# An early run of GpSimd's check, and four low halves of weights moved, in a fused attention and expert layer

## The reference, cut to what matters

```python
sim = jnp.einsum('bhnd,bhmd->bnm', Q, K) / (jnp.sqrt(jnp.float32(d)) * H)
k = max(1, int(n * TOP_K_RATIO))                      # 512 * 0.3
threshold = jax.lax.top_k(sim, k)[0][:, :, -1:]
A = jax.nn.sigmoid(sim) * (sim >= threshold)
A = (A + jnp.swapaxes(A, -1, -2)) * 0.5
x = x + (1 - gamma) * layernorm(x) + gamma * A
...
x = x + moe(layernorm(x)) + shared(layernorm(x))      # 8 experts, 2 per row; shared: silu(x sg + b) * (x su + b) @ sd
```

## Time and profile before

| | |
|---|---|
| runs | 503.43 us median of 3 (503.19 to 504.45) |
| span of the profiled execution | 502.5 us |
| busy: TensorE | 458.7 us (91%) |
| busy: VectorE | 330.9 us (66%) |
| busy: ScalarE | 259.6 us (52%) |
| busy: GpSimd | 148.8 us (30%) |
| mean granted TensorE clock | 0.972 of full |

### The profile page before, as it was taken

How to read it: one execution, slowest core, us unless ns; L and a number is a source line. 1 busy time by engine, 2 the same in 40 slices (tenths; PEclk the granted TensorE clock), 3 DMA queues, 4 the chain that set the end, 5 groups by cost and what they waited for, 6 DMA issues and landing times.

```text
span 502.5 us, 9186 instructions
## 1 busy us (share of the span) xinstructions
PE 458.7 (91%) x2649; PEld 257.1 (51%) x2650; DVE 330.9 (66%) x947; ACT 259.6 (52%) x490; POOL 148.8 (30%) x201
## 2 busy tenths in 40 slices
PE   7529899899999999999989999999999999999960
PEld 2215443455455445554445666666666666666630
DVE  3899989999999999659845555555555433333320
ACT  5899588288627852335445555554545333333320
POOL 3010100031002200410153554555455444444431
PEclk9778999999999999999999999999999999999995
DMA  7931420256023501355397798777777545445441
GB/s 264 277 78 54 136 85 1 83 113 162 0 85 87 83 0 66 109 83 146 107 188 234 187 226 197 181 178 198 176 176 180 87 67 100 83 76 93 82 68 23
DMA packets 39007, 60.55 MB, mean 121 GB/s; under 512 B 8234, under 2 KB 18730, under 8 KB 38963
## 3 DMA queue, kind: packets, MB, share of 16 engines
q0 software_dynamic: 10384, 23.38, 27.3%
q1 hardware_dynamic: 26514, 36.61, 23.1%
q10 hardware_dynamic: 2064, 0.02, 0.2%
HBM read 37.68 MB, written 22.30 MB: 119 GB/s over the span
## 4 chain that ended last, share of the span: by engine, by line
PE 76%; DVE 10%; DMA 4%; ACT 4%; issue 3%; POOL 1%; SPq 0%; DVEq 0%; POOLq 0%; ACTq 0%
PE bank L1055 6%; PE bank L1056 6%; PE bank L1057 6%; PE bank L1234 4%; PE bank L1238 4%; PE bank L1235 4%; PE bank L1210 4%; PE bank L1212 4%; PE bank L1214 4%; PE bank L1213 4%; PE bank L1215 4%; PE bank L1211 4%; PE bank L1067 3%; PE bank L1194 3%; PE bank L1070 3%
## 5 line engine op out<-in xcount | busy, mean ns | idle before, releaser
L567 POOL DMA_INDIRECT out_dram<-xb,sidx x35 | 55.9, 1597 | 83.8 <-ACT xb L905 65.0
L1055 PE MATMUL bank<-xT,W 128*128 128x512 f16 x176 | 66.8, 380 | 0.5 <-DVE sgt L1593 0.5
L1056 PE MATMUL bank<-xT,W 128*128 128x512 f16 x176 | 66.8, 379 | 0.0
L1057 PE MATMUL bank<-xT,W 128*128 128x512 f16 x176 | 66.8, 379 | 0.0
L1726 DVE TENSOR_TENSOR hS<-bank,hS 128x384 f16<-128x384 f32 x35 | 19.4, 556 | 67.9 <-ACT hS L897 67.9
L891 ACT ACTIVATE sgt<-bank 128x352 f32<-128x352 f32 x35 | 16.2, 462 | 72.9 <-PE bank L1215 72.9
L905 ACT ACTIVATE xb<-bank,wcol 128x512 f32<-128x512 f32 x35 | 24.0, 687 | 52.5 <-PE bank L1238 52.5
L1210 PE MATMUL bank<-W,xT 128*128 x140 | 43.8, 313 | 1.5 <-DVE W L1298 1.2
L1214 PE MATMUL bank<-W,xT 128*128 x140 | 43.8, 313 | 0.0
L1211 PE MATMUL bank<-W,xT 128*128 x140 | 43.8, 313 | 0.0
L1212 PE MATMUL bank<-W,xT 128*128 x140 | 43.8, 313 | 0.0
(11 more groups left out here) (263 smaller groups left out, 1022.4 us busy)
## 6 DMA issues: line engine op xcount, KB each, us to landing
out_dram<-W POOLq DMA_DIRECT2D x12, 256.0 KB, 5.1
stage<-L_ffn_down_w_in SPq DMA_DIRECT2D x12, 256.0 KB, 3.6
sim<-L_ffn_down_w_in SPq DMA_DIRECT2D x12, 256.0 KB
stage<-L_ffn_gate_w_in SPq DMA_DIRECT2D x16, 176.0 KB, 3.6
stage<-L_ffn_up_w_in SPq DMA_DIRECT2D x16, 176.0 KB, 4.5
sim<-L_ffn_gate_w_in SPq DMA_DIRECT2D x16, 176.0 KB
sim<-L_ffn_up_w_in SPq DMA_DIRECT2D x16, 176.0 KB
W<-x_in SPq DMA_DIRECT2D x2, 1024.0 KB, 6.8
```

What stands on the lines that cost most here:

```text
L567: pool.indirect_dma_start(out=out, out_offset=bass.IndirectOffsetOnAxis(ap=sidx[:, p:p + 1], axis=0), in_=y2[:, p, :], in_offset=None, com ...
L1055: pe.matmul(o, wh, xT[:, 0, c, :], start=(c == 0), stop=False)
L1056: pe.matmul(o, wh, xT[:, 1, c, :], start=False, stop=False)
L1057: last = pe.matmul(o, wl, xT[:, 0, c, :], start=False, stop=(c == KD - 1))
```

## The change

GpSimd, once its constants are set, runs the check instruction once on two columns of zeros (`bad[:, 2:4]`, used for nothing else). The low halves of units 8 and 9 are formed on TensorE (`form_down_low`, in place of four fillers behind the transposes of batch 0's normalised rows) and rounded by ScalarE (`round_down_low`). Those of units 10 to 13 stand in batch 1, one in each probe. The four squares of batch 1 move on ScalarE from ahead of the last four `round_low` to behind the two new roundings, ahead of the first count of batch 1, and `x_variance(1)` moves behind the low half in probe 0. The counts in the waits (`lows_done`, `s_wloA`) follow.

```diff
+PE_DOWN_LOWS = range(EARLY, EARLY + 2)
...
 def lows_done(n):
 
-    return n - len(PE_LOWS)
+    return n - len(PE_LOWS) - len(PE_DOWN_LOWS)
...
         pool.memset(hS[0:1, 1, SC - 1, :], 1.0).then_inc(s_const, 1)
+        link(pool.memset(bad[:, 2:4], 0.0))
+        pool.partition_all_reduce(bad[:, 3:4], bad[:, 2:3], P, bass.bass_isa.ReduceOp.max)
...
+        def round_down_low(i):
+
+            act.wait_ge(s_lowps, LOW_PARTS + i + 1)
+            lo = UNITS[PE_DOWN_LOWS[i]][2]
+            act.activation(W[:, lo:lo + D], bank[4 + i][:, :], ACT.Copy, scale=WS).then_inc(s_wloA, 1)
...
             x_mean(1)
-            for t in range(TB):
-                x_square(1, t)
             for f in range(4, LOW_PARTS):
                 round_low(f)
...
             x_hi(b, 2)
             x_hi(b, 3)
             if b == 0:
+                for i in range(len(PE_DOWN_LOWS)):
+                    round_down_low(i)
+                for t in range(TB):
+                    x_square(1, t)
                 count(1, 0)
...
+        def form_down_low(i):
+
+            n = PE_DOWN_LOWS[i]
+            pe.wait_ge(s_whi, n - EARLY + 1)
+            hi = UNITS[n][1]
+            pe.matmul(bank[4 + i][:, :], ident[:, :], staged(n)[0], start=True, stop=False)
+            pe.matmul(bank[4 + i][:, :], minus16[:, :], W[:, hi:hi + D], start=False, stop=True).then_inc(s_lowps, 1)
...
             if n == 0:
                 pe.wait_ge(s_wloD, KD)
-                pe.wait_ge(s_wloA, LOW_PARTS)
+                pe.wait_ge(s_wloA, LOW_PARTS + len(PE_DOWN_LOWS))
...
                 pe.wait_ge(s_wloA, LOW_PARTS)
-                keep_on(4)
+                for i in range(len(PE_DOWN_LOWS)):
+                    form_down_low(i)
             logits(b)
...
             if b == 1 and it == 0:
+                copy_logits(0)
+                weight_lo(10)
                 x_variance(1)
-                copy_logits(0)
-                weight_lo(12)
             if b == 1 and it == 1:
                 shared_hidden(0, 0)
                 layer_norm_x(1)
+                weight_lo(11)
             if b == 1 and it == 2:
                 shared_lo(0, 0)
-                weight_lo(13)
+                weight_lo(12)
             if b == 1 and it == 3:
                 shared_hidden(0, 1, lo_first=False)
+                weight_lo(13)
...
             link(dve.tensor_reduce(thr[:, :], pick[:, :, :], AX.X, ALU.add))
-            if b == 0:
-                weight_lo(8)
-                weight_lo(9)
...
-            if b == 0:
-                weight_lo(10)
-                weight_lo(11)
             dve.wait_ge(s_badr, b + 1)
```

## The result

| | before | after |
|---|---|---|
| median of 14 runs each, us | 503.81 (502.82 to 504.48) | 504.76 (503.77 to 505.38) |
| ratio, 95 % interval | | 1.0023 (1.0016 to 1.0030) |
| span of the profiled execution, us | 502.5 | 503.3 |

The changed kernel is slower by 0.23 % in the ratio of the runs, some 1.15 us; the two medians lie 0.95 us apart. I had forecast no visible change, 0.1 us the other way. The time lies in the range, but the direction was wrong. The loss is about the 0.7 to 1.05 us of rival B; B's time of 504.3 counted from the 503.43 of three runs, where the kernel before has 503.81 in fourteen.

A forecast was written before the change was run, and what follows sets the result against it. Bound: engines in turn until 89.66 us, with GpSimd's late check covered by VectorE's low halves, then TensorE. Span 502.5 - 1.17 (batch 0) + 1.05 (batch 1) = 502.38, plus 0.93 around it, 503.3 us; range 501.7 to 505.0.

The forecast's parts named there:

- rival B: GpSimd: each config change reloads the check; batch 0 gains 0 to 0.36, batch 1 loses 1.05; about 504.3 us; chance 0.18.
- Part 1: GpSimd's early run of the check: costs nothing, and batch 0's real check starts at 36.9 us in place of 39.58.
- the later price: GpSimd, batch 0: the check behaves as in later batches, starting right behind its flags at 36.9 us and taking 0.38.
- the other bound: GpSimd, batch 0: latest forecast start of the real check, 39.58 us, as in the kernel before; the early bound was 36.8.
- price of nothing: GpSimd's queue at the start: the early run is covered, free by 12 us, before the first wait ends at 32.36.
- Part 2: Batch 0's threshold without four low halves: VectorE gains 2.77 us, TensorE's fillers hold it to 41.91, batch 0 gains 1.17.
- Part 3: ScalarE, where batch 1's four squares (2.83 us) leave: nothing won, as the rounded parts behind them wait for TensorE.
- Part 4: Two low halves on TensorE and ScalarE: with the squares, batch 1's first count comes 0.9 us late; bounds 0 and 1.2.
- Part 5: VectorE's low halves between batch 1's probes: the one in probe 1 costs 0.15 us; batch 1 loses 1.05 in all.

The follow-up runs named there:

- experiment 1: The changed kernel without GpSimd's early run of the check; ratio to the kernel before 1.0021 (1.0009 to 1.0033).
- Experiment 7: The kernel before with one small GpSimd instruction between flags and check, a product in batch 1 and a memset in batch 2; single run 518.46 us.
- experiment 3: The changed kernel with batch 0's first-norm power left out of GpSimd's queue, VectorE using a straight line instead; ratio to the kernel before 0.9961.
- experiment 5: The changed kernel with VectorE's variance step of batch 0 one tile sooner; ratio to the kernel before 0.9988 (0.9972 to 1.0004).
- experiment 8: The changed kernel with batch 0's variance step one tile sooner and two of batch 1's four squares back in place; ratio to the kernel before 0.9972, median 502.53.
- experiment 4: The changed kernel with batch 1's four squares back ahead of ScalarE's last four rounded low parts; ratio to the kernel before 1.0006 (0.9991 to 1.0022).
- experiment 6: The kernel before with two of the four low halves put ahead of batch 0's flags; ratio to the kernel before 0.9989 (0.9972 to 1.0006).
- experiment 2: The kernel before with GpSimd's early run of the check alone added; ratio to the kernel before 0.9997 (0.9988 to 1.0005).

## Why the prediction was wrong

**Part 1 failed, at one price:** "I take the later price: start right behind the flags, at 36.9". It was 39.91, 0.33 past the other bound, 39.58, and rival B was the right case. (B's gain of 0 to 0.36 us for batch 0 did not come either: it was a loss of 0.14, less than the check's start scatters between traces.) Two readings led me wrong. I took the shorter checks of batches 1 to 3 (0.38 against 0.74 us) as a sign that the code stays loaded; experiment 1 shows a first check of 0.38. And I took prompt checks in batches 1 to 3 as the later price, though I had written that a wait of 19 us and more (18.6 in batch 3) would hide a load. Experiment 7 took that cover away and the load was there. The Trainium skill, GPSIMD Engine Reference, section Instruction dispatch, gives about 6 us for the first call of a freshly loaded kernel. These traces agree, with 5.59 to 6.13 us from the end of the power, and add that the check was fresh again after every config change that no long wait covered. The early run itself ended at 14.66 and not by 12, with a load of 8.94 us; it was covered all the same, so its price of nothing held.

**Part 2** was right as a mechanism and came to nothing with part 1. TensorE's hold by the fillers was seen in experiment 3, and with the check 1.31 us behind its flags (experiment 5) batch 0 gained 1.25 us on before at the transposes; I had 1.23. That the two agree so well is partly luck. I had the fillers end at 41.9 in any case, but they end at 40.94 in the changed kernel's trace, and the gain goes from 0.86 in experiment 3, where they end 5.49 us behind the flags, to 1.34 in experiment 8, where it is 5.00. In the changed kernel itself the term was +0.14 (8.04 against 7.90), where I had -1.17.

**Part 3** held: nothing was won where the squares left (ScalarE then waits 2.67 us for TensorE at 48.46).

```profile
48.46 0.46 ACT L641 ACTIVATE W<-bank 128x352 f16<-128x352 f32 x1 [2.67 <-PE bank L963]
```

**Part 4** held to a tenth. Relative to the probe the first count is 0.9 us late (25.43 - 24.51 = 0.92, against 0.03), as forecast, and 0.04 late when the squares are back (experiment 4). The products on TensorE took what I had scaled from 352 columns, 1.07 to 1.08 each:

```profile
56.49 1.02 PE L970 MATMUL bank<-W,ident 128*128 128x512 f32 x2
57.35 0.38 PE L971 MATMUL bank<-W,minus 128*128 128x512 f16 x1
57.56 1.02 PE L970 MATMUL bank<-W,ident 128*128 128x512 f32 x2
```

**Part 5** was a little high: from the first to the second answer of VectorE's probes it is 4.14 us against 4.11 before, so the low half of probe 1 cost 0.03 in the changed kernel (0.10 in experiment 4) and not 0.15.

```profile
67.94 0.68 DVE L1319 SCALAR_TENSOR_TENSOR W<-W 128x512 f16<-128x512 f32 x1
68.54 0.15 DVE L1434 TENSOR_TENSOR msk<-probe,target 128x4 f32<-128x4 f32 x1
```

With the measured terms the sum is +0.14 for batch 0 and +0.91 for batch 1, together the 1.05 us of the last column.

## What to carry to other kernels

A cost that recurs is invisible wherever a wait covers it, so "only the first one is slow" cannot be read from later instances that had 19 us of cover; take the cover away before using their price. To bring an instruction like the check forward on GpSimd, start its config write sooner, by finishing what stands ahead of it in the queue sooner. Running it once early was worth nothing where an instruction of another kind came between; whether it is worth anything where none does was not tried; by the reading of experiments 5 and 6 the load would then start early by itself. And work that leaves a covered wait must find a gap as wide as itself: 3.89 us did not hold two roundings, the waits between them and four squares.

## What the runs showed that I had not expected

The load begins at the config write, which follows the power within 0.2 us, and runs on while the queue waits for its semaphore: in experiments 5 and 6 the check followed the power by 5.76 and 5.65 us, as in the other kernels, though the flags stood nearer. That a load of code fills the interval is not shown; the traces show its length, and in that of before no DMA packet from 33.5 to 39.5 us.

The early run's load took longer than all the others, 8.0 us (experiment 2) to 9.9 (experiment 3) from the instruction before it, against 5.6 to 6.1 later. It falls into the time in which the first weights arrive (the page's slices show the DMA engines at seven to nine tenths there); that the transfers slow it down was not tried.
